# Per-batch results inside a token-expert stage: tiles listed by the batch in which they begin, results added and stored seven tiles behind

## Chip, core and metric

The kernel runs on one core of one Trainium2 chip. The metric is device time in microseconds (us) of one execution, taken as the median over runs. A profiled execution gives the trace from which all rows below come.

## What is computed

A small vision tower over 8 images of 1024 tokens, 128 wide: token embedding, attention (8 heads), sequence experts, block attention, token experts. Only the last part is touched. Each token is normalised, a router picks 2 of 8 experts for it, and both results, weighted, are added to the token:

```python
top2 = top_k(z @ Wr, 2); g = softmax(top2.values)            # z: normalised x, [8192, 128]
y_e  = gelu(z @ W1[e] + b1[e]) @ W2[e] + b2[e]               # 128 -> 512 -> 128
out  = x + g[0] * y_{e0} + g[1] * y_{e1}
```

## The kernel before

**Block attention** (`block_attention`, from line 1551) goes batch by batch (B = 8). For each batch VectorE (DVE) chooses the experts (`choose`), works out each token's place in its expert's queue (`route`), and GpSimd (POOL) scatters the token rows to `queue` in DRAM with 16 indirect DMAs a batch (L1639). `queue` holds one region for each expert. The counts in each region are known only after the last batch: then `plan` (L1948 to L1984) makes a list of N = 39 tiles of 512 rows, `tile_e` (expert) and `tile_row` (first row), ordered by expert, then row. 32 tiles would hold 16384 rows; partly filled tiles take up to 7 more, and what is left of the 39 are tiles of padding. In the meantime SyncE (SP) writes padding behind each region (8 DMAs, L1616), waits for the plan, loads the weights of the first two tiles (L1620), waits until all rows are scattered, and loads the rows of those two tiles (L1626).

**Token experts** (`token_experts`, from L2008, which calls `expert_items`, L1117) works through the 39 tiles. For tile m:
- SP loads its 512 rows (`load_rows`, L2033, 260 KB, two buffers) and its expert's weights (`load_parts`, L2039, 1026 KB, four buffers). The order on SP is rows(m), weights(m), rows(m+1), weights(m+1) and so on, all in one queue. Weights(m) wait for the output of tile m-4, rows(m) for the turning and the copy of rows(m-2).
- TensorE (PE) in its iteration m turns the rows of tile m+2 (`turn_x`, L1196; it waits for the rows and for `x_lo` of tile m+1), then alternates the first products of tile m+1 and the second products of tile m, each three matmuls (L70 to L72), and turns back the output of tile m-1 (`turn_y`, L1226).
- ScalarE (ACT) applies GELU twice to each of 4 blocks (L1160, L1163), copies the turned rows (L1170), adds the output bias (L1176).
- DVE in its iteration m makes the low parts of tile m+1 in four steps (`low`, L1257). After step 0 it copies two columns of rows(m+3) (`rows_next`, L2064, which waits for these rows), after step 1 it makes `x_lo` of tile m+2 (`split_x`, L1252), and after step 3 it weighs the output of tile m-1 (`weigh`, L2069 and L2070), which waits until the results of tile m-3 have been sent.
- POOL sends each weighed tile to `result` in DRAM with four indirect DMAs (L2051). The destination of a row is fixed by its token and by which of its two experts it was, so that a batch's results lie together, 1 MB. Rows of padding have a place out of bounds and are not written.

**Adding up** (`add_results`, L2080) is a stage of its own, after POOL has seen all sends land and all engines have met. Eight loads of 1 MB (L2093), four issued by SP and four by ACT; for each batch two adds of 128x1024 into H (L2114, L2116); and a store of 512 KB to `out` in pieces of 512 bytes (L2101).

Of the kernel before, what the change touches and what calls it, by code (L numbers as in the profile page):

```python
# [17 lines left out]
P = 128  # L18
# [1098 lines left out]
def expert_items(nc, c, block, N, per_x, ident, w, w_wait, rows, out_func, rows_wait, rows_next, weigh, x_ps, t_ps, t_read, y_done, NB, D, aside=None):  # L1117
# [69 lines left out]

# [60 lines left out]
    def _(dve):  # L1248
# [36 lines left out]
        back(N - 1)  # L1285


class Rest:
# [23 lines left out]
    def turn(self, pe, m):  # L1312
        pe.wait_ge(self.freed, sum(m + 1 >= k for k in self.PE))

# [60 lines left out]
class Ahead:  # L1375


    def __init__(self, nc, ctx, half, ins, B, S, D, E):
# [14 lines left out]
        self.upto, self.steps, self.number = c.sb("upto", [1, E, E]), c.sb("steps", [1, 1, self.M]), c.sb("number", [1, self.N])  # L1393
# [5 lines left out]
        self.W_IN = 16 * 14  # L1399

    def load(self, sp):
        ins = self.ins
        for dst, n in ((self.w_qk[:, :, :], "Wqk"), (self.w_v[:, :], "Wv1"), (self.w_proj[:, :], "Wproj"), (self.w_r[:, :], "Wr"),
                       (self.bcol[:, :], "b_qkv"), (self.rev[:, :, :], "rev"), (self.before[:, :], "before"), (self.base[:, :, :], "base"),
                       (self.place_of[:, :, :], "place_of"), (self.upto[:, :, :], "upto"), (self.steps[:, :, :], "steps"),
                       (self.number[:, :], "number"), (self.pad_place[:, :, :], "pad_place")):
            sp.dma_start(dst, ins[n]).then_inc(self.w_in, 16)
# [143 lines left out]
def block_attention(nc, H, queue, counts, row, idx, sent, rows, rows_in, tile_e, tile_row, parts, w1, w1_in, ident, half, ahead, ins, B, S, D):  # L1551
# [19 lines left out]
    with ExitStack() as ctx:  # L1571
# [3 lines left out]
        place_of, diag, upto, steps, number, pad = ahead.place_of, ahead.diag, ahead.upto, ahead.steps, ahead.number, ahead.pad  # L1575
# [10 lines left out]
        slot, newc = c.sb("slot", [P, K, T]), c.sb("newc", [P, E])  # L1586
# [3 lines left out]
        mark = c.sb("mark", [1, E, M])  # L1590
        tiles, ends = c.sb("tiles", [1, 1, E]), c.sb("ends", [1, 1, E])
        over, part = c.sb("over", [1, N, E]), c.sb("part", [1, N, E])
        e_f, done_f, row_f = (c.sb(n, [1, N]) for n in ("e_f", "done_f", "row_f"))
# [9 lines left out]
         pos_ps, slot_done, n_ps, n_done, planned, padded) = (c.sem(n) for n in (  # L1603
            "cleared var_z root_z x_ps hi_done x_done xt_done qk_ps qk_done v_ps v_done s_ps "
            "sub_done exp_done diag_done o_ps o_done p_ps h_done zn_done z_ps z_done l_ps gap_done ex_done row_done sel_done "
            "pos_ps slot_done n_ps n_done planned padded").split())
# [129 lines left out]
        def _(pe):  # L1736
# [109 lines left out]
            nc.tensor.matmul(psS[:, 0:E], all_ones[:, :], counts[:, :], start=True, stop=True).then_inc(n_ps, 1)  # L1846

        @block.vector
        def _(dve):
# [52 lines left out]
            def choose(n):  # L1902
# [22 lines left out]
                nc.vector.tensor_reduce(newc[:, :], both[:, :, :].rearrange("p t e -> p e t"), AX, ALU.add)  # L1925

            def route(n):
# [14 lines left out]
                nc.vector.tensor_tensor(counts[:, :], counts[:, :], newc[:, :], ALU.add)  # L1942
# [5 lines left out]
            def plan():  # L1948
# [6 lines left out]
                nc.vector.tensor_tensor(mark[:, :, :], n_f[:, 0, :].unsqueeze(2).broadcast_to([1, E, M]), steps[:, :, :].broadcast_to([1, E, M]), ALU.is_gt)  # L1955
                dve.drain()
                nc.vector.tensor_reduce(tiles[:, 0, :], mark[:, :, :], AX, ALU.add)
                dve.drain()
                nc.vector.tensor_tensor(upto[:, :, :], upto[:, :, :], tiles[:, :, :].broadcast_to([1, E, E]), ALU.mult)
# [4 lines left out]
                nc.vector.tensor_tensor(over[:, :, :], ends[:, :, :].broadcast_to([1, N, E]), number[:, :].unsqueeze(2).broadcast_to([1, N, E]), ALU.is_le)  # L1964
                dve.drain()
                nc.vector.tensor_reduce(e_f[:, :], over[:, :, :], AX, ALU.add)
                nc.vector.tensor_tensor(part[:, :, :], over[:, :, :], tiles[:, :, :].broadcast_to([1, N, E]), ALU.mult)
                dve.drain()
                nc.vector.tensor_reduce(done_f[:, :], part[:, :, :], AX, ALU.add)
                dve.drain()  # L1970
                nc.vector.tensor_tensor(row_f[:, :], number[:, :], done_f[:, :], ALU.subtract)
                dve.drain()
                nc.vector.tensor_scalar(row_f[:, :], row_f[:, :], float(CH), None, ALU.mult)
                nc.vector.tensor_scalar(done_f[:, :], e_f[:, :], float(STRIDE), None, ALU.mult)
                dve.drain()
                nc.vector.tensor_tensor(row_f[:, :], row_f[:, :], done_f[:, :], ALU.add)
                dve.drain()
                nc.vector.tensor_scalar(row_f[:, :], row_f[:, :], float(E * STRIDE), None, ALU.min)
                nc.vector.tensor_scalar(e_f[:, :], e_f[:, :], float(E - 1), None, ALU.min)
                dve.drain()  # L1980
                nc.vector.tensor_copy(tile_row[:, :], row_f[:, :])
                nc.vector.tensor_copy(tile_e[:, :], e_f[:, :])
# [25 lines left out]
def token_experts(nc, queue, result, rows, rows_in, tile_e, tile_row, ident, parts, w, w_in, B, S, D):  # L2008
# [8 lines left out]
    with ExitStack() as ctx:  # L2017
# [5 lines left out]
        sent = [c.sem(f"sent{i}") for i in range(2)]  # L2023

# [3 lines left out]
        def _(sp):  # L2028
# [12 lines left out]
            for m in range(2, N):  # L2041
                load_rows(m)
                load_parts(m)

        @block.gpsimd
        def _(pool):
# [6 lines left out]
            for i in range(2):  # L2053
                pool.wait_ge(sent[i], len(range(i, N, 2)) * 16 * TPC)
# [11 lines left out]
        def weigh(dve, psT, m):  # L2066
            if m >= 2:
# [9 lines left out]
                     x_ps, t_ps, t_read, y_done, NB, D)  # L2077


def add_results(nc, H, result, out, B, S, D):  # L2080


    T = S // P
    K = 2
    with ExitStack() as ctx:
        c = Core(nc, ctx, "out")
        y = [c.sb(f"y{b}", [P, K, T, D]) for b in range(B)]
        y_in = [c.sem(f"y_in{b}") for b in range(B)]
        summed, stored = c.sem("summed"), c.sem("stored")
        with nc.Block() as block:  # L2090
            def load(eng, b):
                rows = result[b * K * S:(b + 1) * K * S, :]
                eng.dma_start(y[b][:, :, :, :], rows.rearrange("(p k t) d -> p k t d", p=P, k=K)).then_inc(y_in[b], 16)  # L2093

            @block.sync
            def _(sp):
                for b in range(0, B, 2):
                    load(sp, b)
                for b in range(B):
                    sp.wait_ge(summed, b + 1)  # L2100
                    sp.dma_start(out[b * S:(b + 1) * S, :].rearrange("(t p) d -> p t d", p=P), H[:, b * T:(b + 1) * T, :]).then_inc(stored, 16)  # L2101
                sp.wait_ge(stored, B * 16)

            @block.scalar
            def _(act):
                for b in range(1, B, 2):
                    load(act, b)

            @block.vector
            def _(dve):  # L2110
                for b in range(B):
                    h = H[:, b * T:(b + 1) * T, :]
                    dve.wait_ge(y_in[b], 16)
                    nc.vector.tensor_tensor(h, h, y[b][:, 0, :, :], ALU.add)  # L2114
                    dve.drain()  # L2115
                    nc.vector.tensor_tensor(h, h, y[b][:, 1, :, :], ALU.add).then_inc(summed, 1)  # L2116


def tower(nc, ins, out):
    B, S, D, NH = 8, 1024, 128, 8  # L2120
    nc.disable_value_cache = True
    with ExitStack() as ctx:
# [40 lines left out]
        token_experts(nc, queue, result, rows, rows_in, tile_e, tile_row, ident, experts[1], w1, w1_in, B, S, D)  # L2163
        add_results(nc, H, result, out, B, S, D)


def host(inputs):
# [35 lines left out]
    a["upto"] = np.tril(np.ones((8, 8), np.float32))[None]  # L2203
    a["steps"] = (np.arange(M) * CH).astype(np.float32)[None, None]
    a["number"] = np.arange(N).astype(np.float32)[None]
# [23 lines left out]
```

## Time and profile before

| | |
|---|---|
| median of 3 runs | 1395.64 us (1392.77 to 1396.8) |
| the profiled execution | 1399.67 us, its span 1397.9 us |
| PE busy | 1188.1 us, 85% of the span |
| ACT busy | 996.6 us, 71% |
| DVE busy | 934.3 us, 67% |
| POOL busy | 563.1 us, 40% |
| DMA | 180.58 MB, mean 129 GB/s |
| SP's hardware queue | 129.97 MB, 33.3% of the 16 DMA engines |

All times of rows count from the start of the span. Matmuls are pipelined and their ends are modelled, so that a matmul's own time overlaps the next. The token experts run from about 1085 to 1356 us, adding up from there to the end.

### The profile page before, as it was taken

The numbers are of one execution on the slowest core, as the hardware profiler recorded it, in microseconds if no ns is written. First come the engines' busy times: TensorE is split into PE (matmuls) and PEld (weight loads), VectorE is DVE, ScalarE is ACT, GpSimd is POOL, SyncE is SP. The second block draws the span as 40 slices with busy tenths as digits, with TensorE's granted clock in tenths as the row PEclk, the third lists the DMA queues.
The fourth block names the chain that finished last, engine by engine and source line by source line (L and its number), as shares of the span: only waits on it lengthen the run. The fifth ranks groups of instructions, "written<-read, shape, count | busy, mean of one in ns | idle before, by whom it ended". The sixth has DMA issues, their size and how long they took to land. (4 is left out here: it accounts for less than half of the span.)

```text
span 1397.9 us, 26985 instructions
## 1 busy us (share of the span) xinstructions
PE 1188.1 (85%) x9386; PEld 794.3 (57%) x9386; DVE 934.3 (67%) x2612; ACT 996.6 (71%) x1351; POOL 563.1 (40%) x546
## 2 busy tenths in 40 slices
PE   3799999999999998979989997888971999999930
PEld 2344444444444444437768875777861788888830
DVE  4466868686868686748978885777652566666625
ACT  0598888888888888858868986455420899999930
POOL 3423434333333333210201100177776277776760
PEclk9799999999999999979999999889865899999975
DMA  3673737464645455223211300011115667767619
GB/s 86 121 188 91 190 90 180 99 178 101 172 107 159 117 148 127 84 88 111 86 61 61 100 22 8 5 51 47 49 48 171 208 234 238 245 233 256 218 31 355
DMA packets 93164, 180.58 MB, mean 129 GB/s; under 512 B 15597, under 2 KB 64200, under 8 KB 84960
## 3 DMA queue, kind: packets, MB, share of 16 engines
q1 hardware_dynamic: 73664, 129.97, 33.3%
q0 software_dynamic: 17344, 42.68, 9.3%
q10 hardware_dynamic: 2016, 6.16, 1.4%
q8 instruction: 77, 1.26, 0.4%
q14 instruction: 63, 0.52, 0.1%
HBM read 116.96 MB, written 63.12 MB: 129 GB/s over the span
## 5 line engine op out<-in xcount | busy, mean ns | idle before, releaser
L744 ACT ACTIVATE a_probs<-a_psS 128x1024 f32<-128x1024 f32 x512 | 484.3, 1034 | 93.6 <-PE a_psS L829 59.7
L841 PE MATMUL a_psO<-a_probs,a_v 128*32 128x256 f32 x4096 | 282.9, 395 | 16.9 <-DVE a_o_t L1018 16.5
L1257 DVE TENSOR_TENSOR f_g_lo<-f_g,f_g_hi 128x512 fp32r<-128x512 f32 x284 | 195.2, 689 | 117.4 <-ACT f_g L1163 115.8
L2051 POOL DMA_INDIRECT result<-f_out,f_idx x156 | 181.5, 1164 | 93.7 <-issue 58.7
L841 PEld LDWEIGHTS a_psO<-a_probs,a_v 128*32 128x32 f32 x4096 | 108.9, 111 | 154.2 <-issue 89.7
L1639 POOL DMA_INDIRECT queue<-all_row,all_idx x128 | 126.3, 987 | 38.5 <-issue 37.9
L829 PE MATMUL a_psS<-ag_qs,ag_ks 50*128 50x512 f32 x512 | 97.4, 457 | 9.4 <-issue 5.8
L829 PE MATMUL a_psS<-a_qs,a_ks 50*128 50x512 f32 x512 | 97.4, 456 | 7.5 <-issue 3.5
L402 POOL TENSOR_TENSOR ag_rs_f<-ag_veps_f,all_half 128x4 f32<-128x4 f32 x32 | 33.7, 1054 | 125.9 <-DVE ag_veps_f L99 125.9
L1418 POOL TENSOR_TENSOR ah_rs<-ah_veps,all_half 128x4 f32<-128x4 f32 x16 | 18.5, 1155 | 156.1 <-DVE ah_veps L1431 156.0
L829 PEld LDWEIGHTS a_psS<-ag_qs,ag_ks 50*128 50x128 f32 x512 | 39.9, 191 | 57.4 <-ACT a_probs L744 31.3
L829 PEld LDWEIGHTS a_psS<-a_qs,a_ks 50*128 50x128 f32 x512 | 39.5, 189 | 55.1 <-ACT a_probs L744 37.4
L713 POOL DMA_DIRECT2D experts<-a_split x32 | 19.7, 615 | 110.0 <-DVE a_split L1036 110.0
L1160 ACT ACTIVATE f_g_hi<-f_psH,ag_qs 128x512 fp32r<-128x512 f32 x72 | 50.2, 697 | 15.5 <-PE f_psH L72 15.0
L1160 ACT ACTIVATE f_g_hi<-f_psH,all_w 128x512 fp32r<-128x512 f32 x76 | 53.1, 698 | 10.2 <-PE f_psH L72 9.5
L1160 ACT ACTIVATE f_g_hi<-f_psH,f_w 128x512 fp32r<-128x512 f32 x64 | 44.6, 697 | 20.4 <-PE f_psH L72 19.5
L1160 ACT ACTIVATE f_g_hi<-f_psH,ag_ks 128x512 fp32r<-128x512 f32 x72 | 50.2, 698 | 8.9 <-PE f_psH L72 8.0
L1163 ACT ACTIVATE f_g<-f_psH,all_w 128x512 f32<-128x512 f32 x76 | 53.0, 698 | 0.0
L1163 ACT ACTIVATE f_g<-f_psH,ag_ks 128x512 f32<-128x512 f32 x72 | 50.2, 698 | 0.0
L1163 ACT ACTIVATE f_g<-f_psH,ag_qs 128x512 f32<-128x512 f32 x72 | 50.1, 696 | 0.0
L1196 PE MATMUL f_psX<-all_ident,all_rows 128*128 128x128 f32 x156 | 24.4, 280 | 27.9 <-DMA all_rows<-queue 26.4
L1226 PE MATMUL f_psT<-all_ident,f_y 128*128 128x128 f32 x284 | 42.8, 273 | 5.3 <-issue 2.9
(370 smaller groups left out, 2866.2 us busy)
## 6 DMA issues: line engine op xcount, KB each, us to landing
all_w<-experts SPq DMA_DIRECT2D x19, 1026.5 KB, 5.3
experts<-a_split POOLq DMA_DIRECT2D x32, 512.0 KB, 4.9
ag_qs<-experts SPq DMA_DIRECT2D x14, 1026.5 KB, 5.4
ag_ks<-experts SPq DMA_DIRECT2D x14, 1026.5 KB, 5.2
all_rows<-queue SPq DMA_DIRECT2D x39, 260.0 KB, 5.4
f_w<-experts SPq DMA_DIRECT2D x8, 1026.5 KB, 5.3
qparts<-a_parts SPq DMA_DIRECT2D x16, 512.0 KB, 3.6
kparts<-a_parts SPq DMA_DIRECT2D x14, 512.0 KB, 3.2
```

The costliest lines, as they stand in the source:

```text
L402: self.nc.gpsimd.tensor_tensor(self.rs_f[:, :], self.veps_f[:, :], half[:, 0:TPC], ALU.pow).then_inc(self.root_f, 1)
L713: pool.dma_start(experts[stage][e, :, 2 * layer * HID:2 * (layer + 1) * HID], split[:, :, :].rearrange("p a h -> p (a h)").bitcast(F32)).t ...
L744: nc.scalar.activation(probs[u % NPR][:, :], psS[score_buffer(u)][:, :, :].rearrange("p a n -> p (a n)"), ACT.Exp).then_inc(exp_done, 1)
L829: last = nc.tensor.matmul(psS[score_buffer(u)][:, p, :], ks[par][64 * p:64 * p + KG, kt, hp * P:(hp + 1) * P], queries(par, hp, p, a), sta ...
L841: last = nc.tensor.matmul(psO[32 * g:32 * g + 32, a * HALF:(a + 1) * HALF], v[par][:, 2 * hp + p, kt, :], probs[u % NPR][:, cols:cols + HA ...
L1160: nc.scalar.activation(g_hi[i][:, n, :], psH[n][:, :], ACT.Gelu, bias=bias(m, n))
L1163: nc.scalar.activation(g[:, n, :], psH[n][:, :], ACT.Gelu, bias=bias(m, n)).then_inc(g_done, 1)
L1196: last = nc.tensor.transpose(psX[:, i * P:(i + 1) * P], rows(m)[:, i, 0:D], ident[:, :])
L1226: last = nc.tensor.transpose(psT[:, i * P:(i + 1) * P], y[m % 2][:, i * P:(i + 1) * P], ident[:, :])
L1257: nc.vector.tensor_tensor(g_lo[i][:, n, :], g[:, n, :], g_hi[i][:, n, :].bitcast(F32), ALU.subtract).then_inc(lo_done, 1)
L1639: pool.indirect_dma_start(queue, bass.IndirectOffsetOnAxis(ap=idx[n % NROW][:, k, t:t + 1], axis=0), row[n % NROW][:, k, t, :], None).then ...
L2051: pool.indirect_dma_start(result, bass.IndirectOffsetOnAxis(ap=idx[i][:, j:j + 1], axis=0), out[i][:, j, :], None, bounds_check=2 * B * S ...
```

## The change

`plan` lists the tiles by the batch in which they begin, and by expert within it. For that it needs the counts after each batch and not only at the end: 16 small matmuls give them on 8 partitions, one for each batch; DVE then works out each batch's tiles: after the copy of the counts to `n_i`, which stays, 27 instructions on 8 partitions (two of them behind one more matmul, which adds the eight partitions' answers) take the place of 16 on one partition. The constants are widened to 8 partitions, and one small table (`since`) is loaded with the others.

The stage `add_results` is gone. Its work moves into `token_experts`, as class `Adds`, through the hooks that `expert_items` already has for the sequence experts. At most FULL[b] = 4(b+1) + 7 tiles begin in batches 0 to b (11, 15, 19, 23, 27, 31, 35, 39). When SP has issued rows and weights of tile m = FULL[b] + 7 (18, 22, 26, 30, 34, 38 for b = 0 to 5), it stores batch b-1 and loads the results of batch b. DVE adds them in its iteration of the same number m. Batches 6 and 7 are handled at the end, the last one in halves, and its second half of loading and storing is issued by ACT. Two buffers of an earlier stage (`n0`, `f`) take the results. POOL no longer waits at the end.

```diff
@@ expert_items, scalar
+        aside.act_end(act)
@@ expert_items, vector
         back(N - 1)
+        if aside is not None:
+            aside.close(dve)
@@ block_attention, tensor
             nc.tensor.matmul(psS[:, 0:E], all_ones[:, :], counts[:, :], start=True, stop=True).then_inc(n_ps, 1)
+            for i in range(2):
+                for n in range(B):
+                    last = nc.tensor.matmul(psX[0][0:B, i * E:(i + 1) * E], since[:, i, n, :], newc[:, n, :], start=(n == 0), stop=(n == B - 1))
+            last.then_inc(n_ps, 1)
+            pe.wait_ge(sums_done, 1)
+            nc.tensor.matmul(psX[1][0:1, 0:2 * N], all_ones[0:B, 0:1], both_f[:, :, :].rearrange("b i m -> b (i m)"), start=True, stop=True).then_inc(tile_ps, 1)
@@ plan
                 nc.vector.tensor_copy(n_i[:, :], n_f[:, 0, :]).then_inc(n_done, 1)
-                nc.vector.tensor_tensor(mark[:, :, :], n_f[:, 0, :].unsqueeze(2).broadcast_to([1, E, M]), steps[:, :, :].broadcast_to([1, E, M]), ALU.is_gt)
...
+                dve.wait_ge(n_ps, 2)
+                nc.vector.tensor_copy(upto_b[:, :, :], psX[0][0:B, 0:2 * E].rearrange("b (i e) -> b i e", e=E))
+                for i in range(2):
+                    dve.drain()
+                    nc.vector.tensor_tensor(mark[:, :, :], upto_b[:, i, :].unsqueeze(2).broadcast_to([B, E, M]), steps[:, :, :].broadcast_to([B, E, M]), ALU.is_gt)
+                    dve.drain()
+                    nc.vector.tensor_reduce(tiles[i][:, 0, :], mark[:, :, :], AX, ALU.add)
+                dve.drain()
+                nc.vector.tensor_tensor(fresh[:, :, :], tiles[0][:, :, :], tiles[1][:, :, :], ALU.subtract)
...
+                nc.vector.tensor_tensor(over[:, :, :], ends[:, :, :].broadcast_to([B, N, E]), count, ALU.is_gt)
+                nc.vector.tensor_tensor(part[:, :, :], begin[:, :, :].broadcast_to([B, N, E]), count, ALU.is_gt)
...
+                dve.sem_inc(sums_done, 1)
+                dve.wait_ge(tile_ps, 1)
+                nc.vector.tensor_scalar(tile_row[:, :], psX[1][0:1, 0:N], float(E * STRIDE), None, ALU.add)
+                nc.vector.tensor_copy(tile_e[:, :], psX[1][0:1, N:2 * N])
                 dve.drain()
                 dve.sem_inc(planned, 1)
@@ class Adds
+        self.FULL = [min(self.K * S // CH * (b + 1) + N - self.K * B * S // CH, N) for b in range(B)]
+        self.LAG = 7
+
+    def load(self, eng, b, parts=(0, 1)):
+        rows = self.result[b * self.K * self.S:(b + 1) * self.K * self.S, :].rearrange("(p k t) d -> p k t d", p=P, k=self.K)
+        for i in range(2):
+            eng.wait_ge(self.sent[i], (self.FULL[b] + 1 - i) // 2 * 16 * TPC)
+        if b >= 2:
+            eng.wait_ge(self.summed, b - 1)
+        for k in parts:
+            eng.dma_start(self.y[b % 2][k][:, :, :], rows[:, k, :, :]).then_inc(self.y_in[b % 2], 16)
+
+    def store(self, eng, b):
+        T, S = self.T, self.S
+        eng.wait_ge(self.summed, b + 1)
+        eng.dma_start(self.out[b * S:(b + 1) * S, :].rearrange("(t p) d -> p t d", p=P), self.H[:, b * T:(b + 1) * T, :]).then_inc(self.stored, 16)
...
+    def sync(self, sp, m):
+        for b in range(self.B - 2):
+            if m == self.FULL[b] + self.LAG:
+                if b:
+                    self.store(sp, b - 1)
+                self.load(sp, b)
+
+    def sync_end(self, sp):
+        B = self.B
+        self.load(sp, B - 2)
+        self.store(sp, B - 3)
+        self.store(sp, B - 2)
+        self.load(sp, B - 1, (0,))
+        self.store_half(sp, B - 1, 0)
+        sp.wait_ge(self.stored, (B + 1) * 16)
+
+    def act_end(self, act):
+        self.load(act, self.B - 1, (1,))
+        self.store_half(act, self.B - 1, 1)
...
+    def add(self, dve, b, k):
+        h = self.H[:, b * self.T:(b + 1) * self.T, :]
+        if k == 0:
+            dve.wait_ge(self.y_in[b % 2], (b // 2 + 1) * 32)
+        else:
+            dve.drain()
+        return self.nc.vector.tensor_tensor(h, h, self.y[b % 2][k][:, :, :], ALU.add)
+
+    def dve(self, dve, m, n):
+        for b in range(self.B - 2):
+            if m == self.FULL[b] + self.LAG:
+                if n == 0:
+                    self.add(dve, b, 0)
+                elif n == 2:
+                    self.add(dve, b, 1).then_inc(self.summed, 1)
+
+    def close(self, dve):
+        b = self.B - 2
+        self.add(dve, b, 0)
+        self.add(dve, b, 1).then_inc(self.summed, 1)
+        b += 1
+        dve.wait_ge(self.y_in[b % 2], (b // 2 + 1) * 32)
+        for half_ in range(2):
+            tiles = slice(half_ * TPC, (half_ + 1) * TPC)
+            h = self.H[:, b * self.T + half_ * TPC:b * self.T + (half_ + 1) * TPC, :]
+            self.nc.vector.tensor_tensor(h, h, self.y[b % 2][0][:, tiles, :], ALU.add)
+            dve.drain()
+            self.nc.vector.tensor_tensor(h, h, self.y[b % 2][1][:, tiles, :], ALU.add).then_inc(self.summed, 1)
@@ token_experts, sync
                 load_rows(m)
                 load_parts(m)
+                adds.sync(sp, m)
+            adds.sync_end(sp)
@@ token_experts, gpsimd
-            for i in range(2):
-                pool.wait_ge(sent[i], len(range(i, N, 2)) * 16 * TPC)
@@
-def add_results(nc, H, result, out, B, S, D):
...
```

## Rows read from the trace of the kernel before

**Rows 1.** Busy time by stage: stretch, its length, PE, PEld, DVE, ACT, POOL; clock, DMA share, GB/s.

```profile
1110.00:1320.00 210.00, 210.00 (x1046) 172.47 (x1045) 132.07 (x260) 192.58 (x326) 153.87 (x131) 1.00 0.71 241
...
1370.00:1380.00 10.00, 0.00 (x0) 0.00 (x0) 9.67 (x9) 0.00 (x0) 0.00 (x0) 0.50 1.01 423
...
1390.00:1398.00 8.00, 0.00 (x0) 0.00 (x0) 0.00 (x0) 0.00 (x0) 0.00 (x0) 0.50 0.86 250
```

**Rows 2.** The chain of work that ended last: start, length, what.

```profile
1362.16 22.83 DMA out_y<-result
```

**Rows 3.** Timeline of the end: start, length, engine, line, operation, [idle before it].

```profile
1344.41 0.98 POOL L2051 DMA_INDIRECT result<-f_out,f_idx  x1 [0.31 <-issue]
...
1346.75 0.17 DVE L2069 COPY f_idx<-f_meta 128x4 int32<-128x4 int32 x1 [4.71 <-DMA result<-f_out,f_idx]
...
1354.67 0.98 POOL L2051 DMA_INDIRECT result<-f_out,f_idx  x1 [0.30 <-issue]
1360.84 2.01 SPq L2093 DMA_DIRECT2D out_y<-result  x4
...
1371.72 21.36 SPq L2101 DMA_DIRECT2D out<-all_H  x8
...
1388.76 1.23 DVE L2116 TENSOR_TENSOR all_H<-all_H,out_y 128x1024 f32<-128x1024 f32 x1
```

**Rows 4.** SP's issues in the steady stretch of the token experts, one tile and the next.

```profile
1204.19 0.33 SPq L2039 DMA_DIRECT2D ag_qs<-experts  x1
1205.33 0.33 SPq L2033 DMA_DIRECT2D all_rows<-queue  x1
1210.64 0.33 SPq L2039 DMA_DIRECT2D ag_ks<-experts  x1
```

**Rows 5.** DMA issues: KB each, median us from issue to landing; last, L1626 alone.

```profile
all_w<-experts SPq DMA_DIRECT2D x19, 1026.5 KB, 5.3
...
all_rows<-queue SPq DMA_DIRECT2D x39, 260.0 KB, 5.4
...
DMA to landing us min/median/max: 2.8/2.8/2.8
```

**Rows 6.** Timeline of DVE and PE around the use of the rows issued at 1205.33.

```profile
1212.90 0.17 DVE L2064 COPY f_meta<-all_rows 128x8 f32<-128x8 f32 x1
...
1213.45 0.69 DVE L1257 TENSOR_TENSOR f_g_lo<-f_g,f_g_hi 128x512 fp32r<-128x512 f32 x1 [0.38 <-ACT f_g L1163]
...
1214.06 0.68 DVE L1252 TENSOR_TENSOR f_x_lo<-f_psX,f_x_hi 128x512 fp32r<-128x512 f32 x1
...
1215.58 0.60 PE L1196 MATMUL f_psX<-all_ident,all_rows 128*128 128x128 f32 x4
```

**Rows 7.** POOL's sends, all of 1110 to 1340 (busy, mean ns), and two single ones.

```profile
L2051 POOL DMA_INDIRECT result<-f_out,f_idx x144 | 169.8, 1179 | 89.7 <-issue 54.7 <-DVEq L2072 35.0
...
1201.82 0.68 DVE L1257 TENSOR_TENSOR f_g_lo<-f_g,f_g_hi 128x512 fp32r<-128x512 f32 x1
1201.86 1.50 POOL L2051 DMA_INDIRECT result<-f_out,f_idx  x1 [0.30 <-issue]
...
1214.25 0.98 POOL L2051 DMA_INDIRECT result<-f_out,f_idx  x1 [0.30 <-issue]
```

**Rows 8.** Timeline of the plan and of SP until the first tiles' rows are loaded.

```profile
1053.27 3.10 PE L1818 MATMUL a_psR<-a_both,ah_all_ones 128*128 128x56 f32 x14
...
1058.62 0.15 DVE L1951 COPY a_n_f<-a_psS 1x8 f32<-1x8 f32 x1 [0.71 <-PE a_psS L1846]
...
1059.76 8.60 SPq L1616 DMA_DIRECT2D queue<-ah_pad  x8
...
1063.53 0.17 DVE L1982 CAST all_tile_e<-a_e_f 1x39 int32<-1x39 f32 x1
...
1069.18 0.36 SPq L1620 DMA_DIRECT2D ag_qs<-experts  x1
...
1082.29 0.86 SPq L1626 DMA_DIRECT2D all_rows<-queue  x2
```

More of the change, by code:

```diff
@@ L1585, in block_attention @@
         top, first_, gap, ex, den = c.sb("top", [P, K, T]), c.sb("first", [P, K, T]), c.sb("gap", [P, T]), c.sb("ex", [P, T]), c.sb("den", [P, T])
-        slot, newc = c.sb("slot", [P, K, T]), c.sb("newc", [P, E])
+        slot, newc = c.sb("slot", [P, K, T]), c.sb("newc", [P, B, E])
         norm_z = c.sb("stat_z", [P, T, 6]), c.sb("mv_z", [P, T, 2]), c.sb("veps_z", [P, T]), c.sb("rs_z", [P, T])
         n_f, n_i = c.sb("n_f", [1, 1, E]), c.sb("n_i", [1, E], I32)
[L1590 to L1593, printed above, removed]
+        upto_b = c.sb("upto_b", [B, 2, E])
+        mark = c.sb("mark", [B, E, M])
+        tiles = [c.sb(f"tiles{i}", [B, 1, E]) for i in range(2)]
+        fresh, ends, begin, off = (c.sb(n, [B, 1, E]) for n in ("fresh", "ends", "begin", "off"))
+        open_ = c.sb("open", [B, 1])
+        over, part = c.sb("over", [B, N, E]), c.sb("part", [B, N, E])
+        hits, both_f = c.sb("hits", [B, N]), c.sb("both_f", [B, 2, N])
         psX = [c.ps(f"psX{i}", [P, CH]) for i in range(2)]
@@ L1962, in plan @@
                 dve.drain()
-                nc.vector.tensor_tensor(over[:, :, :], ends[:, :, :].broadcast_to([1, N, E]), number[:, :].unsqueeze(2).broadcast_to([1, N, E]), ALU.is_le)
+                nc.vector.tensor_scalar(ends[:, 0, :], ends[:, 0, :], open_[:, :], None, ALU.add)
                 dve.drain()
-                nc.vector.tensor_reduce(e_f[:, :], over[:, :, :], AX, ALU.add)
-                nc.vector.tensor_tensor(part[:, :, :], over[:, :, :], tiles[:, :, :].broadcast_to([1, N, E]), ALU.mult)
+                nc.vector.tensor_tensor(begin[:, :, :], ends[:, :, :], fresh[:, :, :], ALU.subtract)
@@ L1977, in plan @@
                 dve.drain()
[L1978 to L1979 removed]
+                nc.vector.tensor_reduce(hits[:, :], over[:, :, :], AX, ALU.add)
+                nc.vector.tensor_tensor(part[:, :, :], over[:, :, :], off[:, :, :].broadcast_to([B, N, E]), ALU.mult)
                 dve.drain()
[L1981 removed]
@@ L2011, in token_experts @@
+def token_experts(nc, H, queue, result, out_rows, y, rows, rows_in, tile_e, tile_row, ident, parts, w, w_in, B, S, D):
     E, _, WIDE = parts.shape
@@ L2023, in token_experts @@
         sent = [c.sem(f"sent{i}") for i in range(2)]
+        adds = Adds(nc, c, H, result, out_rows, y, sent, B, S, D, N)
         block = ctx.enter_context(nc.Block())
@@ L2076, in token_experts @@
         expert_items(nc, c, block, N, 1, ident, lambda m: w[m % NW], w_wait, lambda m: rows[m % 2], ACT.Identity, rows_wait, rows_next, weigh,
-                     x_ps, t_ps, t_read, y_done, NB, D)
-def add_results(nc, H, result, out, B, S, D):
[L2083 to L2116, printed above, removed]
+                     x_ps, t_ps, t_read, y_done, NB, D, adds)
 def tower(nc, ins, out):
@@ L2162, in tower @@
             block_attention(nc, H, queue, counts, row, idx, sent, rows, rows_in, tile_e, tile_row, experts[1], w1, w1_in, ident, half, ahead, ins, B, S, D)
-        token_experts(nc, queue, result, rows, rows_in, tile_e, tile_row, ident, experts[1], w1, w1_in, B, S, D)
-        add_results(nc, H, result, out, B, S, D)
+        token_experts(nc, H, queue, result, out, (shared.n0, ahead.f), rows, rows_in, tile_e, tile_row, ident, experts[1], w1, w1_in, B, S, D)
 def host(inputs):
@@ L2202, in host @@
     a["place_of"] = (np.arange(128)[:, None, None] * K * t + np.arange(K)[:, None] * t + np.arange(tiles) // t * K * S + np.arange(tiles) % t).astype(np.int32)
-    a["upto"] = np.tril(np.ones((8, 8), np.float32))[None]
-    a["steps"] = (np.arange(M) * CH).astype(np.float32)[None, None]
-    a["number"] = np.arange(N).astype(np.float32)[None]
+    a["upto"] = np.tile(np.tril(np.ones((8, 8), np.float32)), (b, 1, 1))
+    a["steps"] = np.tile((np.arange(M) * CH).astype(np.float32), (b, 1, 1))
+    a["number"] = np.tile(np.arange(N).astype(np.float32), (b, 1))
+    first, then = np.meshgrid(np.arange(b), np.arange(b), indexing="ij")
+    a["since"] = np.tile(np.stack([first <= then, first < then]).astype(np.float32), (128, 1, 1, 1))
     a["pad_place"] = np.tile((K * b * S + np.arange(128)).astype(np.int32)[:, None, None], (1, 4, 1))
```

60 lines of the change are left out of this document (43 added, 17 removed).

## The prediction, made before the changed kernel ran

> **What bounds the kernel now.** I read the stages first. From 1110 to 1320 us, well inside the token experts, PE is busy all of 210 us at the full clock, ACT 92% of it, POOL 73%, DVE 63%, and the DMA engines carry 241 GB/s at a share of 0.71 [rows 1]. So this stage goes at PE's pace, and only what makes PE wait can lengthen it. Its period is that of SP's issues, 1210.64 - 1204.19 = 6.45 us a tile [rows 4].
>
> Then the chain that ended last: one link, 22.83 us, is a wait of DVE for the loads of results [rows 2]. The timeline around it [rows 3] gives the end piece by piece. POOL's last send starts at 1354.67. Eight loads are issued from 1360.84 on, the last add starts at 1388.76 and ends at 1389.99, and the span ends at 1397.9. In this time PE, ACT and POOL do nothing and the DMA engines are full (share 1.01, 423 GB/s while it is mostly loads; 0.86, 250 GB/s while only stores are left) [rows 1]. The end costs 1397.9 - 1354.67 = 43.2 us behind the last send's start, nearly all of it DMA traffic that could have run earlier beside PE, if the DMA engines' free 0.29 takes it.
>
> **The end, after the change.** Seven batches leave it; batch 7 stays, since it needs all 39 tiles.
> - Last send to load: at 1346.75 DVE is released by the sends of the tile whose last send started at 1344.41, so a send lands 2.3 us after its start [rows 3]. The loads of batch 7 can go at 1354.67 + 2.3 + 0.1 = 1357.1, not at 1360.84: 3.7 us for POOL's wait and the meeting of all engines fall away.
> - Load of 1 MB by two queues: a 260 KB load on quiet engines lands in 2.8 us [rows 5]; the other 0.78 MB at 423 GB/s take 1.9. That is 4.7 us, to 1361.8. Bounds: 4 and 6.
> - Adds: four of 128x512. A DVE operation of this size takes 0.69 [rows 6], half of 1.23 [rows 3] and a start. Both halves: to 1364.6.
> - Last half store, 256 KB in pieces of 512 bytes: 2.8 us for 260 KB [rows 5], and as stores are slower (250/0.86 = 290 GB/s against 423) 0.3 more: 3.1, at most the 5.4 or so of a load that stands behind another [rows 5]. I take 3.7, as the first half is still under way: 1368.4, and 0.4 to the end of the span, 1368.8.
>
> That is 1397.9 - 1368.8 = **29.1 us saved**, 27 to 30 by the bounds. Batch 6's adds (2 x 1.23) run on DVE while POOL sends tile 38 (4 sends, 5.1 us), and its load and store in the same time; without that cover they would cost 2.5 us. Batch 5's adds come in DVE's iteration 38, before the weighing of tile 37, where DVE had to wait for sends anyway (4.71 us before tile 38's [rows 3]).
>
> **Inside the stage: the added traffic.** Behind weights(m) for m = 18, 22, 26, 30, 34, 38 SP now puts a load of 1 MB and, from the second on, a store of 512 KB. On average that is 1.57 MB in four tiles: 2.5 us for the load (at 423 GB/s) and 1.8 for the store (at 290), 4.3 us in 25.8, so the share goes from 0.71 to 0.88. On average it fits. But rows(m+1) now stand behind it in SP's queue. In the trace rows issued 1.13 us behind weights land in 5.4 us, and on quiet engines in 2.8 [rows 4, 5]: they already wait for what is before them. Rows issued at 1205.33 land at about 1210.7; DVE copies their columns at 1212.90 [rows 6], 2.2 us in hand. With 4.3 to 4.6 us of traffic before them they land at 1215.2, and DVE stands at `rows_next` for 2.3 us. Behind it in DVE's order are one low part (start to start 0.61) and `x_lo` (0.68) [rows 6]: `x_lo` is done at 1215.2 + 0.2 + 0.6 + 0.7 + 0.1 = 1216.8, and PE's next turning of rows, at 1215.58 [rows 6], waits for it. **PE loses 1.3 us**, four times (m = 22, 26, 30, 34): 5.2 us. At m = 18 there is no store: rows at 1213.3, `x_lo` at 1214.9, nothing lost. At m = 38 no rows follow. The bounds of this unknown: 0 where DMA engines take the load in the gaps, 3.5 each (14) where load and store in competition with sends take 1.5 times as long. I take 5.2, nearest to the measured rates. Weights(m+1) are not late: issued at 1210.64, landing by 1219, needed two periods after weights(m) would have been, at 1222.
>
> The Trainium skill ("DMA: Bandwidth & Descriptors", Queues, rings and completion order) says that each DMA engine takes one queue's descriptors in ring order. By that rule the rows can't pass the load, as reckoned; without it the sum would be 5.2 us better. The trace agrees so far: 5.4 against 2.8.
>
> **SP's new waits.** Behind them stand all rows and weights. The load of batch b waits for sends of FULL[b] tiles, that is up to tile m-8. DVE weighs tile m-6 only when tile m-8 has been sent, and weighs it about one period before SP is at m, so this wait is met already. `summed` for the store was raised three to four tiles earlier. Cost 0; it would cost once tile m-8's sends landed more than 6 us later than now. SP's three more issues, 0.33 each [rows 4], lie within the 4.2 us that it waits between rows and weights.
>
> **DVE's adds.** Two of 1.23 us [rows 3] in six iterations. DVE idles 37% of the stage; the first add comes before a low part and `x_lo`, and there DVE had 0.4 us idle and `x_lo` 0.8 us in hand (done 1214.74, needed 1215.58) [rows 6]: 1.23 against 1.2, just hidden. The load is there some three tiles earlier. What they do to POOL is less plain: a send that starts just behind a low part takes 1.50 us, one beside `x_lo`, which reads PSUM, 0.98 [rows 7]; the mean is 1.18 and 0.3 lie between sends, so POOL needs 4 x 1.48 = 5.9 of 6.45 us. An add may hold a send by up to 1.1 us; two in four tiles give 1 to 2 us against 4 x 0.5 = 2.1 to spare. I take **1 us** in all (0 to 6), for tiles where DVE then waits for a send.
>
> The Trainium skill ("SBUF — State Buffer", SBUF: two separate sides) has DVE operations with two SBUF inputs and GpSimd shut each other out of a shared port for a whole instruction. The adds have two SBUF inputs, so it speaks against the change at this place, and the trace agrees with it: 1.50 against 0.98.
>
> **The plan.** It starts at 1058.62 and ends at 1063.7, 18 instructions, 0.28 us each. Added before it: 16 matmuls of two passes, at 3.10/14 = 0.22 a pass 7.1 us; instead of 16 instructions 27, 7.6 us in all; and about 1.8 for a matmul and the handovers (0.71 for the one shown). So it ends at 1075.1. SP is busy with padding until 1059.76 + 8.60 = 1068.4 and issues the first weights 0.8 later; they would go at 1075.9, 6.7 us later. The rows can't go before POOL's last scatter, 1082.29 [rows 8]. Two weight loads of 1 MB need some 7 us there, until 1083 to 1084, and the rows landed at 1085.1. So the cover, POOL's scattering, just suffices: **0**, up to 3 if the matmuls or the weights are slower, never a gain. Without that cover it would be 11 us. The order of tiles changes no size: 39 tiles, each with its own weight load as before.
>
> **Sum.** -29.1 + 5.2 + 1 + 0 = -22.9 against the profiled execution: 1399.67 - 22.9 = 1376.8. That execution is 4.0 above the median of 1395.64, so 1372.8, **1373 us** as a median.
>
> **Rivals.**
> - *The burst costs nothing* (25%): rows come in time, as weights use only 0.71 of the engines and DVE catches up. 1395.6 - 29.1 + 0.5 = 1367. For it: PE busy 210 of 210, DVE's 37% idle. Against: only 2.2 us in hand.
> - *The stage is slowed more* (17%): rows 3.5 us late each time, or sends that let DVE wait again and again: 10 to 16 us, 1377 to 1384.
> - *POOL becomes the bound; slower than before* (4%). From tile 18 on a send plus its gap need only reach 6.45/4 = 1.61 us, 1.31 for the send, to set the pace; single ones have 1.50 [rows 7]. With 21 tiles left it eats the gain of 29 when each tile takes 1.38 more, a send of 1.65 us. At 1.8 us a tile takes 8.4: +41 - 29, 1408. Against: only two of sixteen sends meet an add, and the others have the same DVE work beside them as now.
> - *It doesn't do what it says* (4%): SP's waits hold the early loads so that they pile up at the end, and time stays at about 1394.
>
> The forecast itself has 50%. A measurement of this kernel can tell about 0.3% (4 us) from no change. Faster by more than that: the first three cases and half of the last, 0.95; within it 0.02; slower 0.03. The range, 1364 to 1384: from no stall at all and a run 2 us low, to 14 us of stalls with 2 more in the end.
>
> **What the changed profile would show.** Right: from the last send's start to the end of the span 14 us, not 43; DMA share in the stage near 0.88; DVE idle before L2064's copy on rows 2 to 3 us in four tiles, and PE idle of 1.3 us there; first rows still issued near 1082. Wrong: no idle of PE at these places (then 1367); POOL's sends over 1.3 us on average, with DVE waiting for them; a later start of the experts' first tile; or loads of batches 0 to 5 landing only after 1345.

## The result and the profile after

The changed kernel takes 1375.77 us (median of 4 runs, 1371.32 to 1385.34) against 1396.22 of the kernel before on the same chip: ratio 0.9862, 95% interval 0.9825 to 0.9899. That is 20.4 us, where 22.9 were forecast. The profiled execution took 1371.32 us, its span is 1369.1. It is a lucky one of its kernel: 9.2 us of its lead arise before POOL's last scatter, in code that the change hardly touches; how much such executions differ there is told with the experiments. So the comparison of the two traces is made by parts.

| part, us | before | after | difference | forecast |
|---|---|---|---|---|
| start to the last scatter's start | 1079.5 | 1070.3 | -9.2 | 0, not of the change |
| last scatter to first copy of columns (L2064 before, L2190 after) | 5.5 | 5.4 | -0.1 | 0 |
| first copy to the last send (L2051, L2179) | 269.7 | 280.7 | +11.0 | +6.2 |
| last send to the end of the span | 43.2 | 12.7 | -30.5 | -29.1 |

The last three rows sum to -19.6, and this fits the 20.4 of the medians.

**The end.** Timeline from the last send on, where [rows 3] has the old one:

```profile
1356.35 0.98 POOL L2179 DMA_INDIRECT result<-f_out,f_idx  x1 [0.30 <-issue]
1358.51 0.34 SPq L2064 DMA_DIRECT2D ah_f<-result  x1
1358.51 0.35 ACTq L2064 DMA_DIRECT2D ah_f<-result  x1
1363.43 0.69 DVE L2128 TENSOR_TENSOR all_H<-all_H,ah_f 128x512 f32<-128x512 f32 x1 [12.08 <-DMA ah_f<-result]
1364.20 0.69 DVE L2130 TENSOR_TENSOR all_H<-all_H,ah_f 128x512 f32<-128x512 f32 x1
...
1364.92 0.37 SPq L2075 DMA_DIRECT2D out<-all_H  x1
1365.57 0.69 DVE L2130 TENSOR_TENSOR all_H<-all_H,ah_f 128x512 f32<-128x512 f32 x1
1366.29 0.43 ACTq L2075 DMA_DIRECT2D out<-all_H  x1
```

The loads go 2.2 us behind the start of the last send, not 6.2. They have landed 4.9 us later, the adds take 2.8, and the last half store is in 2.8 us after its issue.

**The stage.** Busy time by stretch: PE, PEld, DVE, ACT, POOL, then clock, DMA share and GB/s (compare [rows 1]).

```profile
1110.00:1320.00 210.00, 202.09 (x993) 164.74 (x992) 135.43 (x258) 183.26 (x311) 140.84 (x125) 0.99 0.77 267
```

PE, which was busy all of 210 us, now idles 7.9. The waits of the stage, from 1090 to 1345, say for what:

```profile
DVE f_meta L2190 <- DMA all_rows<-queue: 15.5, 5, 4.4
...
PE f_psX L1197 <- DVE f_x_lo L1253: 7.9, 4, 2.8
```

DVE waited five times for rows (the fifth is at m = 18, where no store goes with the load, and PE lost nothing), PE four times for `x_lo`; before, neither wait was there. One of the four places, SP's issues first:

```profile
1207.54 0.33 SPq L2165 DMA_DIRECT2D all_w<-experts  x1
1207.92 0.63 SPq L2069 DMA_DIRECT2D out<-all_H  x1
1208.65 1.44 SPq L2064 DMA_DIRECT2D ah_f<-result  x2
1211.35 0.34 SPq L2159 DMA_DIRECT2D all_rows<-queue  x1
1213.97 0.34 SPq L2165 DMA_DIRECT2D all_w<-experts  x1
...
1220.42 0.33 SPq L2165 DMA_DIRECT2D ag_qs<-experts  x1
...
1228.85 0.33 SPq L2165 DMA_DIRECT2D ag_ks<-experts  x1
```

and DVE and PE (timeline of all engines):

```profile
1219.34 0.17 DVE L2190 COPY f_meta<-all_rows 128x8 f32<-128x8 f32 x1 [3.49 <-DMA all_rows<-queue]
1219.42 0.69 DVE L1258 TENSOR_TENSOR f_g_lo<-f_g,f_g_hi 128x512 fp32r<-128x512 f32 x1
...
1220.02 0.68 DVE L1253 TENSOR_TENSOR f_x_lo<-f_psX,f_x_hi 128x512 fp32r<-128x512 f32 x1
...
1220.85 0.63 PE L1197 MATMUL f_psX<-all_ident,all_rows 128*128 128x128 f32 x4 [1.78 <-DVE f_x_lo L1253]
```

Read together: the rows issued at 1211.35 come 3.8 us behind their weights, not 1.14 [rows 4], since three issues stand between and SP spends 0.63 and 1.44 us on them; they land at about 1219.3, 8 us after their issue and not 5.4 [rows 5]. DVE idles 3.49, makes `x_lo` at once, and PE has lost 1.78. The interval of SP's weight issues (it follows ACT's outputs) shows the loss: 6.45 becomes 8.43 from 1220.42 to 1228.85. Of the 34 intervals behind the start of the stage just four are long: 8.43, 10.97, 8.23, 8.45. They exceed 6.45 by 10.3 us in all, and that is nearly all of the stage's +11.0.

The interval of 10.97 is worth a look, since PE's wait in it was 2.76 only. Windows of the same kind as above:

```profile
1240.00:1245.00 5.00, 5.00 (x26) 4.06 (x25) 2.26 (x5) 4.95 (x10) 3.28 (x4) 1.00 1.04 385
1245.00:1250.00 5.00, 2.24 (x16) 1.66 (x13) 1.91 (x5) 2.53 (x5) 2.89 (x3) 1.00 1.02 402
1250.00:1252.00 2.00, 2.00 (x10) 1.57 (x8) 1.33 (x4) 0.97 (x2) 0.00 (x0) 0.72 1.02 335
1252.00:1254.00 2.00, 2.00 (x6) 1.63 (x5) 0.80 (x2) 1.28 (x3) 1.55 (x2) 0.50 0.83 298
1254.00:1256.00 2.00, 2.00 (x10) 1.56 (x10) 1.20 (x2) 1.45 (x4) 1.39 (x3) 0.93 0.24 87
```

PE was busy only 2.24 of 5 us, and the granted clock then fell from 1.00 to 0.50 (from 2.4 to 1.2 GHz) for some 3 us. A wait of 2.8 us cost 4.5, while the waits of the other three long intervals (1.8, 1.6, 1.8 us) cost each 0.2 more than itself. The DMA engines were full until the clock had fallen (1.04, 1.02).

**The plan.** Timeline, for [rows 8]:

```profile
1049.28 0.96 PE L1862 MATMUL a_psX<-a_newc,ah_since 128*8 128x8 f32 x32
...
1050.27 0.16 DVE L1975 COPY a_upto_b<-a_psX 8x16 f32<-8x16 f32 x1 [0.50 <-PE a_psX L1862]
...
1050.52 8.53 SPq L1629 DMA_DIRECT2D queue<-ah_pad  x8
...
1058.78 0.17 DVE L2020 CAST all_tile_e<-a_psX 1x39 int32<-1x39 f32 x1
...
1059.91 0.36 SPq L1633 DMA_DIRECT2D ag_qs<-experts  x1
...
1073.03 0.86 SPq L1639 DMA_DIRECT2D all_rows<-queue  x2
```

It is ready at 1058.95, just as SP ends its padding at 1059.05. The first weights go 0.86 us after that, before 0.82. The plan isn't even late for the weights, let alone for the rows.

### The profile page after: what moved, and what is told of

Same layout as the page of the kernel before. It is cut to its first block and busy times, and to the rows that moved or that the text cites. A ratio compares the mean times of both kernels' runs of the same rounds, so it can differ in the third digit from the quotient of the medians.

```text
span 1369.1 us, 27080 instructions
## 1 busy us (share of the span) xinstructions
PE 1184.1 (86%) x9420; PEld 793.2 (58%) x9420; DVE 934.1 (68%) x2625; ACT 994.5 (73%) x1351; POOL 558.9 (41%) x546
## 5 line engine op out<-in xcount | busy, mean ns | idle before, releaser
L841 PE MATMUL a_psO<-a_probs,a_v 128*32 128x256 f32 x4096 | 279.6, 391 | 17.8 <-DVE a_o_t L1018 17.4
L2179 POOL DMA_INDIRECT result<-f_out,f_idx x156 | 176.5, 1131 | 109.6 <-DVEq L2198 59.8
L1160 ACT ACTIVATE f_g_hi<-f_psH,all_w 128x512 fp32r<-128x512 f32 x76 | 53.0, 697 | 20.4 <-PE f_psH L72 11.0
L1160 ACT ACTIVATE f_g_hi<-f_psH,ag_qs 128x512 fp32r<-128x512 f32 x72 | 50.1, 696 | 15.6 <-PE f_psH L72 15.1
```

The costliest lines, as they stand in the source:

```text
L841: last = nc.tensor.matmul(psO[32 * g:32 * g + 32, a * HALF:(a + 1) * HALF], v[par][:, 2 * hp + p, kt, :], probs[u % NPR][:, cols:cols + HA ...
L2179: pool.indirect_dma_start(result, bass.IndirectOffsetOnAxis(ap=idx[i][:, j:j + 1], axis=0), out[i][:, j, :], None, bounds_check=2 * B * S ...
```

## The experiments

Theory Q: rows stand behind up to 1.5 MB in SP's queue, come late to DVE, and PE waits for `x_lo`. Rival A: DVE's adds, or what they do to POOL's sends. Rival T: the DMA engines are full, whatever the order. And one run for the plan alone. Total times of the changed kernel scatter with a standard deviation of about 0.5%, mostly from the part before the experts (the first copy of columns came between 1075.7 and 1091.8 us in executions that have the same code up to the plan). The kernels ran on several chips, each beside the kernel before; rows first, three pieces, no adds and the plan alone had no changed kernel beside them. So besides the ratio each verdict rests on the trace: the stage (first copy of columns to last send), and "excess", the sum by which SP's intervals between weights exceed 6.45 us once the stage is under way. The excess ends with the last weights; behind them each kernel without the separate adding stage loses another 0.3 to 3.6 us, the difference between its stage and 269.7 plus its excess. One trace was taken of each.

| kernel | ratio to before, 95% | stage, us | excess, us | wait for rows, for x_lo (us, times) |
|---|---|---|---|---|
| before | 1 | 269.7 | 0 | none |
| changed | 0.9862 (0.9825 to 0.9899) | 280.7 | 10.3 | 15.5 (5), 7.9 (4) |
| changed, again | 0.989 (0.9851 to 0.993) | 280.4 | 9.9 | 15.1 (5), 7.5 (4) |
| rows first | 0.9824 (0.9767 to 0.9881) | 274.3 | 2.9 | 2.1 (2), 0.4 (1) |
| three pieces | 0.9826 (0.976 to 0.9893) | 276.2 | 4.2 | 5.7 (4), 4.7 (4) |
| no adds | 0.9882 (0.9816 to 0.9948) | 279.9 | 9.9 | 13.9 (5), 7.5 (4) |
| plan alone | 1.0023 (0.9987 to 1.0059) | 271.0 | 1.3 | none |
| issued by ACT | 0.9854 (0.9825 to 0.9883) | 278.2 | 4.9 | 0.7 (1), 5.6 (6) |
| no store in the stage | 0.9775 (0.9745 to 0.9805) | 274.4 | 3.1 | 8.2 (5), 2.1 (4) |
| rows first, three pieces | 0.9813 (0.9794 to 0.9833) | 272.1 | 0.4 | none, 1.2 (1) |
| the same, again | 0.9801 (0.9759 to 0.9843) | 273.6 | 1.6 | 1.1 (2), 1.3 (1) |
| rows first, half loads, stores last | 0.9819 (0.9785 to 0.9853) | 271.9 | 0.5 | 0.3 (1), 0.3 (1) |

**Rows first.**

```diff
                 load_rows(m)
+                adds.sync(sp, m - 1)
                 load_parts(m)
-                adds.sync(sp, m)
+            adds.sync(sp, N - 1)
```

> Each batch's store and load are issued one place later on SP: behind the rows of the next tile, ahead of its weights. Nothing else changes. Theory Q (the four stalls of the changed kernel come from rows that stand behind 1.5 MB in SP's queue): the rows are issued 1.1 us after the weights again and land in 5 to 6 us, no wait for x_lo over 0.5 us on PE at m = 22, 26, 30, 34, stage shorter by 8 to 10 us, ratio to before 0.979. Rival A (the 128x1024 adds on DVE and what they do to POOL's sends cost it): no change against the changed kernel, 0.986. Rival T (the DMA engines are simply full): the stalls move to the weights or to the next tile's rows and stay at 6 to 10 us, 0.985.

Moving the burst by one place takes 7.4 of 10.3 us of excess away, and 6.4 us of the stage where 8 to 10 were expected; the bytes and the adds are as they were. The ratio, 0.9824, is above the expected 0.979; its interval holds that, and overlaps that of the changed kernel, so it is the trace that shows the gain. One long interval remains, 9.05 us, and it has another cause:

```profile
1297.61 0.98 POOL L2180 DMA_INDIRECT result<-f_out,f_idx  x1 [6.07 <-issue]
...
1306.52 0.17 DVE L2196 COPY f_idx<-f_meta 128x4 int32<-128x4 int32 x1 [4.79 <-DMA result<-f_out,f_idx]
...
1307.43 0.63 PE L1227 MATMUL f_psT<-all_ident,f_y 128*128 128x128 f32 x4 [2.40 <-DVE f_out L2197]
```

POOL paused for 6.07 us between two sends with nothing shown that held it; the sends came late, so did the weighing, so did PE's turning. The pause is no accident of this execution. In all twelve traces of the table POOL stands still before the same send, the second of tile 28: 4.5 to 6.1 us in eight of them, the kernel before among these (4.5, without cost), and 2.0 us in the other four (the changed kernel both times, no adds, no store in the stage), where POOL had stood idle for 2.1 to 3.2 us just before, waiting for DVE. So where no stall comes just before it, the pause comes out at its full length, and in the kernels with the rows first most of the excess that is left lies behind it. What it is stays open.

**Three pieces**, at the old place.

```diff
-            if m == self.FULL[b] + self.LAG:
-                if b:
-                    self.store(sp, b - 1)
-                self.load(sp, b)
+            step = m - self.FULL[b] - self.LAG
+            if step == 0:
+                if m == self.N - 1:
+                    self.store(sp, b - 1)
+                    self.load(sp, b)
+                else:
+                    self.load(sp, b, (0,))
+            elif step == 1:
+                self.load(sp, b, (1,))
+            elif step == 2 and b:
+                self.store(sp, b - 1)
```

> The burst is spread over three tiles: half of the load, the other half, the store, each 512 KB behind its own tile's weights (batch 5, at the last tile, stays as it is). Same bytes. Theory Q: 512 KB are 1.2 to 1.8 us, under the 2.2 us that the rows have in hand, so no stall, or one of 0.5 us where a weight load runs at the same time: ratio 0.979 to 0.981. Rival A: 0.986. Rival T: 0.983 to 0.986, as the same bytes pass in the same stage.

Worse than expected (0.979 to 0.981 and no stall): 0.9826, and 4.2 us of excess in three intervals. The timeline shows why.

```profile
1232.55 0.17 DVE L2197 COPY f_meta<-all_rows 128x8 f32<-128x8 f32 x1 [1.33 <-DMA all_rows<-queue]
1232.63 1.22 DVE L2116 TENSOR_TENSOR all_H<-all_H,ah_f 128x1024 f32<-128x1024 f32 x1
...
1235.26 0.63 PE L1197 MATMUL f_psX<-all_ident,all_rows 128*128 128x128 f32 x4 [0.91 <-DVE f_x_lo L1253]
```

The rows behind the store are 1.33 us late, by itself about what DVE has in hand before `x_lo` (0.4 + 0.8, [rows 6]); but the late rows now fall in the tile in which DVE does its first add, between the copy and `x_lo`, and 1.33 + 1.22 is more. So an add does cost when the rows are late. In the changed kernel the two fall in different tiles.

**No adds in the stage** (12 DVE instructions of batches 0 to 5 are left out).

```diff
-                    self.add(dve, b, 0)
+                    dve.wait_ge(self.y_in[b % 2], (b // 2 + 1) * 32)
                 elif n == 2:
-                    self.add(dve, b, 1).then_inc(self.summed, 1)
+                    dve.sem_inc(self.summed, 1)
```

> Leaves out the in-stage adds of batches 0 to 5 (12 instructions of 128x1024 on DVE), so that these batches are stored without the experts' results; loads, stores and waits are as in the changed kernel. Theory Q: the four stalls stay (about 2 us of PE each), the time is that of the changed kernel less at most 1 us: ratio 0.985. Rival A: the stalls go, 0.979, and the mean of POOL's sends falls.

All four long intervals stay, 9.9 against 10.3 us, and POOL's sends take no less, 1.15 us on average against 1.13. Rival A falls.

What an add does to a send can be seen in the changed kernel, near the end, where POOL is otherwise undisturbed at 0.98:

```profile
1348.81 2.53 DVE L2109 TENSOR_TENSOR all_H<-all_H,ag_n 128x1024 f32<-128x1024 f32 x2
1349.47 1.41 POOL L2179 DMA_INDIRECT result<-f_out,f_idx  x1 [0.31 <-issue]
```

0.43 us for one send that starts within an add, which POOL's spare time takes.

**The plan alone**: `plan` and its matmuls as changed, token experts and `add_results` as before.

> Only the new plan, with the separate adding stage of before. If the longer plan hides behind POOL's scattering, as in the changed kernel's trace (rows issued 2.7 us behind the last scatter, before 2.8), the ratio is 1.000, within 0.002; the order of the tiles changes nothing in the stage (269.7 us from the first copy of columns to the last send, within 1). If the plan costs or the new order of experts makes weight loads slower, 1.002 to 1.006.

The ratio's interval holds 1. The stage is 1.3 us longer, where at most 1 was expected. The rows go out 2.8 us behind the last scatter; the 1.3 us are two intervals at the very end (7.37 and 6.81), 11 us behind POOL's pause, here of 5.8 us. In the 210 us from 1110 on PE is busy for 209.24 us, so the new order of experts costs the weight loads nothing.

**Issued by ACT**, in a queue of its own, at the same time.

```diff
             output(m)
+            aside.act(act, m)
...
+    def act(self, act, m):
+        self.sync(act, m + 4)
...
                 load_parts(m)
-                adds.sync(sp, m)
```

> The in-stage stores and loads of batches 0 to 5 are issued by ACT behind the output of the same tile, at the same time, so in a queue of their own; bytes and times stay. Theory Q: the rows no longer wait for the whole burst; they share the engines with it instead, so they land 2 to 3 us earlier than in the changed kernel and the four waits for x_lo shrink to under 1 us each. ACT loses 1 to 2 us for its own issues each time, in six tiles, of which it has 0.5 us to spare: 3 to 8 us come back in. Ratio 0.984 to 0.988. Rival T: the waits for rows stay as they are, since the engines are full whatever the queue; ratio 0.988 to 0.992.

The waits of DVE and PE in this kernel, 1105 to 1345:

```profile
ACT f_g_hi L1160 <- DMA result<-f_out,f_idx: 6.6, 4, 1.7
PE f_psX L1198 <- DVE f_x_lo L1254: 5.6, 6, 1.6
...
DVE f_meta L2196 <- DMA all_rows<-queue: 0.7, 1, 0.7
```

This tells Q from T: same bytes at the same time on the same engines (share 0.80 from 1120 to 1320, changed kernel 0.78), and the wait for rows falls from 15.5 us to 0.7. At the four bursts the rows land 6.3 to 6.8 us after their issue, in the changed kernel 7.8 to 9.3. One thing besides the queue changed with this edit: in the changed kernel SP spends some 2 us on the three issues, and the rows are issued 2.3 to 2.7 us later behind their weights than before; with ACT issuing, that falls away too. The three pieces tell the two apart: there the four late rows were issued only 0.5 us later, and still landed 8.1 to 8.7 us after their issue. So the place in the queue does make rows late by itself; how much the later issue adds in the changed kernel isn't shown.

What PE still waits has another source: ACT lost 1.7 us at each of the four bursts to its own waits and issues, and four intervals are 7.4 or 7.5 us. Two more, 7.10 and 6.77, come behind POOL's pause, and 3.6 us are lost behind the last weights.

**No store in the stage**: the stores of batches 0 to 4 are issued behind the load of batch 6.

```diff
-                if b:
-                    self.store(sp, b - 1)
                 self.load(sp, b)
...
         self.load(sp, B - 2)
+        for b in range(B - 3):
+            self.store(sp, b)
         self.store(sp, B - 3)
```

> The stores of batches 0 to 4 leave the stage and are issued at its end, so that each burst is the load of 1 MB alone. Theory Q: the wait grows with the bytes ahead of the rows: 2.5 us instead of 4.3, so the four long tiles shrink to under 1 us over 6.45 each, as at m = 18. The end grows by 2.5 MB of stores in part beside POOL's last sends: 2 to 6 us. Ratio 0.982 to 0.986. Rival A (adds on DVE): four tiles stay 2 us longer.

With 1 MB ahead of the rows and not 1.5 the excess falls from 10.3 to 3.1, as Q says. The expected cost at the end isn't there: last send to end is 12.6 us. SP issues the stores from 1339 us on, while POOL sends the last tiles, and they are through before the last send at 1359. The ratio, 0.9775, is the lowest of all, below the 0.982 to 0.986 that was expected; the stage of the trace, 274.4 us, doesn't explain why it should lie under that of rows first, and this stays open.

**Rows first and three pieces**, both edits.

> Both edits together: three pieces of 512 KB in three tiles, each behind the rows of the next tile and ahead of its weights. Theory Q: rows never stand behind a piece, and weights have over 6 us in hand, so the stage has the length of before (269.7 us from the first copy of columns to the last send) within 2 us, and the time is 9 us under that of the changed kernel: ratio to before 0.978 to 0.980. Rival T (full DMA engines also slow POOL's sends, on which DVE waits): one or two tiles longer by 2 us or more remain, stage 273 to 276 us, 0.982.

Its window from 1120 to 1320, in the columns of [rows 1]:

```profile
1120.00:1320.00 200.00, 199.90 (x990) 163.31 (x988) 134.71 (x255) 183.25 (x311) 139.49 (x124) 1.00 0.83 280
```

PE is busy again nearly all the time, with the DMA share at 0.83, the highest of all kernels, where the kernel before has 0.71. Rival T falls a second time: the engines have room for it all. On the same chip the changed kernel took 1382.26 us and this one 1372.63; the intervals of their ratios (0.9851 to 0.993 and 0.9794 to 0.9833) don't meet. Its expectations were just missed: the stage is 272.1 us, 2.4 over that of before where 2 were allowed, and the ratio 0.9813, not 0.978 to 0.980. That is nearer to the numbers that were given for rival T (273 to 276 us, 0.982), but rows no longer wait, and the one interval of note (6.72) comes behind POOL's pause, here of 4.8 us.

The changed kernel beside it:

> The changed kernel once more, beside the others of this call. Theory Q: again four tiles longer than 6.45 us, at m = 23, 27, 31, 35, by 1.7 to 4.5 us, 8 to 11 us in all; ratio to before 0.984 to 0.988.

Again four long intervals (8.39, 8.69, 8.15, 10.47), and again in one of them the clock fell: 1.00 until 1315, 0.54 and 0.61 in the next two stretches of 2 us. PE's wait there was 2.3 us and cost 4.0.

**Rows first, loads in halves, stores last**, and beside it the kernel with three pieces again.

> Loads in two halves, one tile apart, each behind the next tile's rows and ahead of its weights; the stores of batches 0 to 4 are issued behind the last load of the loop, when few transfers are left. Theory Q: no wait for rows at all, stage 270 to 272 us but for what the stores do to the last sends (0 to 2 us), the end 12.6 us as in the kernel with the stores out of the stage: ratio to before 0.975 to 0.979, and equal to or up to 2 us under the kernel with three pieces. Rival T: sends late behind the stores, one tile longer by 3 us or more near the end: 0.981.

> The kernel with three pieces of 512 KB behind the rows once more, on the same chip as the one with the stores last: ratio to before 0.979 to 0.983 (0.9813 the first time), stage 272 us.

1369.76 and 1367.2 us: no difference that can be told, and the ratio for the stores last, 0.9819, is above the expected 0.975 to 0.979, though stage (271.9 us) and end (12.8) came as expected. With the rows first, no effect of the place of the stores is left to see. Both beat the kernel before and, by the stage (272 to 274 against 281 us), the changed one.

## Why the prediction was right, point by point

- **The end**, -29.1: measured -30.5. The wait of POOL and the meeting of engines, 4.0 us (3.7 reckoned), and the load, 4.9 from issue to the first add (4.7), came as worked out; the last half store landed in 2.3 us by the trace and not in 3.7, most of the difference.
- **The burst before the rows**, +5.2: right in its place, its number (four tiles, none at m = 18 and m = 38) and its chain (rows, copy, low part, `x_lo`, PE). Its size was the term that failed: 10.3 us, twice the forecast. Two parts of it. PE's waits for `x_lo` sum to 7.9 us, 2.0 each and not 1.3: in the tile shown the rows landed 0.7 us later than reckoned (1219.3 against 1215.2 shifted by 3.35, as the weights went at 1207.54 and not at 1204.19), in the worst one more. Over the four tiles the rows landed 11.6 to 12.8 us behind their weights, 5.1 to 6.2 us later than the 1.14 and 5.4 of before add up to, where about 4.5 was reckoned. The other 2.4 us are mostly the fall of the clock in that worst tile, which lost 4.5 us by a wait of 2.8; the step had no such term. The bounds, 0 to 14, held it.
- **The share of the DMA engines** was to rise to 0.88 and was 0.77 from 1110 to 1320 us, 0.79 from 1200 on, where the bursts run (before 0.72). The sign failed, and the rows were late all the same.
- **The ring order**: the rows waited for the burst. The Trainium skill ("DMA: Bandwidth & Descriptors", Queues, rings and completion order) has each DMA engine take the descriptors of one queue in the order of its ring, and gives SP and ACT a ring each on every engine. The traces agree: with the burst in ACT's queue the wait for rows is 0.7 us and not 15.5.
- **SP's new waits**, 0: right. SP issued store and loads 0.4 and 1.1 us behind the weights. But the issues themselves were not 0.33 us each: store and loads took 0.63 and 1.44 us in the tile shown, and the rows went out 2.7 us later behind their weights than before.
- **DVE's adds**, +1: within what can't be told from 0 (9.9 us of excess without them, 10.3 with). Batch 5's adds in DVE's iteration 38 were put at nothing, since DVE had to wait for sends there. In the trace they delayed the weighing of tile 37 (1343.10 us, right behind 2.53 us of adds), and PE then waited 2.0 us, before 1.0; POOL, with sends still to do, hid most of it: the stage lost 0.7 us behind its last weights.
- **The plan**, 0: right, for a partly wrong reason. The 27 instructions took about 8 us (7.6 reckoned), but the 16 matmuls 0.96 us and not 7.1, as the price of matmuls with 128 columns of weights was put on some with 8. It ended with the padding and never came near its second cover, the scattering.
- **The sum**, 1373 against 1375.8: the cost of the burst was put 5 us too low, the gain at the end 1.4 too low and the adds 1 too high. So the total is nearer than its largest term, and part of that is luck: two errors took back half of the third. (Slips in the sums, 1368.8 for 1368.7 and 0.95 for 0.94, change nothing.)

The rival "the stage is slowed more" (17%) described the stage better than the forecast did: it named rows 3.5 us late each time and 10 to 16 us, and DVE's four waits were 2.8 to 4.4 us, 3.5 on average, the stage 11.0 longer. Its total, 1377 to 1384, was missed by 1 us, by what the end and the adds gave back. The rival "the burst costs nothing" is refuted by the trace, "POOL becomes the bound" too: its sends have a mean of 1.13 us after, 1.16 before, over all 156.

## What to carry to other kernels

When background transfers are put into a stage that a compute engine bounds, the average share of the DMA engines isn't the question; ask what is issued next in the same queue, and how many microseconds it has in hand. Issue them behind the transfer with the least slack and ahead of the one with the most: one moved line took 7 of 10 us of excess away here, by the traces. And look for the end of the stage, where the DMA engines have little to do: five more stores issued there left the time behind the last send as it was.

## What the runs showed of the hardware

- Two-pass fp32 matmuls with weights of 8 columns and 8 columns moving took 0.03 us a pass (32 in 0.96 us); with weights of 128 columns and 56 to 8 moving 0.22 (14 in 3.10), both at a granted clock of 0.50.
- In three traces (the changed kernel twice, no adds once) the granted clock fell once from 1.00 to 0.50 for about 3 us, behind the longest wait of PE in the steady stage, of 2.8, 2.3 and 2.2 us; the wait then cost 1.7 to 1.8 us more than itself. Waits of 2.0 us and less in the same traces were not followed by a fall, but neither was one of 2.4 us in the kernel with the rows first, so the length of the wait alone doesn't decide it.
- POOL stood still before the same send, the second of tile 28, in all twelve traces, with no releaser shown: 4.5 to 6.1 us in eight, 2.0 in the four in which it had just waited for DVE. Only where DVE then waits does it cost.
